# The message stage of a two-layer graph network: GpSimd issues its scatters and gathers by pairs of blocks

## What is computed

```python
h = jnp.maximum(_layernorm(x, axis=-1), 0.0)
src_full = jnp.concatenate([src, dst])
dst_full = jnp.concatenate([dst, src])
ef_full = jnp.concatenate([ef, ef], axis=0)
edge_in = jnp.concatenate([nf[src_full], nf[dst_full], ef_full], axis=-1)
msg = leaky_relu(edge_in @ We1) @ We2
red = jax.ops.segment_sum(msg, dst_full, num_segments=nf.shape[0])
node_in = jnp.concatenate([nf, red], axis=-1)
out_nf = leaky_relu(node_in @ Wn1) @ Wn2
```

## Time and profile before

| | |
|---|---|
| median of 3 runs | 5537.8 us |
| lowest and highest | 5531.38 and 5540.8 us |
| the profiled execution: its time | 5538.13 us |
| its span, first to last instruction | 5536.3 us |
| GpSimd (POOL) busy in the span | 3890.5 us (70%) |
| VectorE (DVE) busy | 3895.1 us (70%) |
| TensorE (PE) busy | 3325.0 us (60%) |
| ScalarE (ACT) busy | 1426.1 us (26%) |
| TensorE's granted clock, mean | 0.795 of full speed |
| scatters of the message stage, L1529 | 831, 1323.0 us, mean 1592 ns |
| gathers of the message stage, L1543 | 832, 828.4 us, mean 996 ns |
| the queue of GpSimd's transfers (q0) | 396.10 MB, 35.3% of the 16 DMA engines' span |

### The profile page before, as it was taken

How to read it: one execution, slowest core, us unless ns; L and a number is a source line. 1 busy time by engine, 2 the same in 40 slices (tenths; PEclk the granted TensorE clock), 3 DMA queues, 4 the chain that set the end, 5 groups by cost and what they waited for, 6 DMA issues and landing times. The chain is left out here.

```text
span 5536.3 us, 106419 instructions
## 1 busy us (share of the span) xinstructions
PE 3325.0 (60%) x16923; PEld 2273.1 (41%) x16924; DVE 3895.1 (70%) x11905; ACT 1426.1 (26%) x2966; POOL 3890.5 (70%) x3803
## 2 busy tenths in 40 slices
PE   0062222222156676244687877877887878778868
PEld 0031111111046665233354554545555545455537
DVE  4635555555578888887587777777777777777765
ACT  0130000000056666433322222222222222222222
POOL 3127777777679999721378888888878787888870
PEclk9685555555567778577899999999999999999989
DMA  2266666666256666412688888888888888888874
GB/s 57 60 182 194 193 196 192 194 194 193 81 126 153 154 155 154 150 42 76 183 183 182 179 180 179 180 179 179 178 177 182 177 180 177 180 179 182 177 144 141
DMA packets 725012, 891.72 MB, mean 161 GB/s; under 512 B 123241, under 2 KB 555465, under 8 KB 724710
## 3 DMA queue, kind: packets, MB, share of 16 engines
q0 software_dynamic: 217200, 396.10, 35.3%
q1 hardware_dynamic: 450742, 392.89, 24.9%
q10 hardware_dynamic: 56976, 101.87, 6.0%
HBM read 652.36 MB, written 238.06 MB: 161 GB/s over the span
## 5 line engine op out<-in xcount | busy, mean ns | idle before, releaser
L1529 POOL DMA_INDIRECT sums<-msg_bsum,k_sidx x831 | 1323.0, 1592 | 285.5 <-issue 241.7
L731 POOL DMA_INDIRECT max_xe<-rows,l_index x832 | 800.6, 962 | 426.6 <-issue 253.3
L1543 POOL DMA_INDIRECT msg_ga<-ab,k_bsrc x832 | 828.4, 996 | 368.7 <-issue 200.1
L1631 ACT ACTIVATE msg_low_ps<-msg_xs 128x512 f32<-128x512 f32 x928 | 558.0, 601 | 1986.8 <-DVE msg_xs L1600 1971.6
L1666 PEld LDWEIGHTS msg_both_ps<-msg_onehot,msg_hid 128*128 128x128 f32 x3712 | 552.0, 206 | 1216.7 <-DVE msg_bsum L1573 688.0
L1679 PE MATMUL msg_pre_ps<-msg_rw,msg_lt 128*128 128x512 f32 x1856 | 1030.0, 638 | 8.9 <-DMA msg_rw<-ab 8.9
L1666 PE MATMUL msg_both_ps<-msg_onehot,msg_hid 128*128 128x64 f32 x3712 | 616.4, 292 | 511.6 <-DVE msg_bsum L1573 500.4
L942 POOL TENSOR_SCALAR att_keyhot<-k_ramp,att_keys 128x128 f32<-128x128 f32 x1028 | 702.0, 703 | 56.1 <-ACT att_keys L1014 54.5
L1610 DVE TENSOR_TENSOR msg_hid<-msg_xs,msg_low_ps 128x512 f32<-128x512 f32 x928 | 634.5, 684 | 88.4 <-ACT msg_low_ps L1631 69.9
L1668 PE MATMUL msg_both_ps<-msg_hid,msg_same 128*128 128x256 f32 x1856 | 654.3, 437 | 0.0
L1599 DVE TENSOR_TENSOR msg_xs<-msg_pre_ps,msg_ga 128x256 f32<-128x256 f32 x928 | 388.9, 419 | 362.4 <-issue 157.4
(11 more groups left out here) (292 smaller groups left out, 5351.3 us busy)
## 6 DMA issues: line engine op xcount, KB each, us to landing
msg_rw<-ab SPq DMA_DIRECT2D x928, 128.0 KB
l_outside<-xe SPq DMA_DIRECT2D x1028, 72.0 KB, 2.7
xe<-max_xe SPq DMA_DIRECT2D x104, 576.0 KB, 3.0
max_src<-srcs ACTq DMA_DIRECT2D x104, 512.0 KB, 3.8
att_keyrow<-key ACTq DMA_DIRECT2D x257, 128.0 KB, 3.5
msg_lt<-in_efT SPq DMA_DIRECT2D x928, 32.0 KB
rows<-node_rows SPq DMA_DIRECT2D x50, 288.0 KB, 2.4
max_begin<-begin ACTq DMA_DIRECT2D x104, 128.0 KB, 2.5
```

Source lines behind the costliest of these rows:

```text
L731: pool.indirect_dma_start(xe[:, b, u, :], None, T.rows, bass.IndirectOffsetOnAxis(ap=K.index[:, k:k + 1], axis=0)).then_inc(s_xe[b], 16)
L1529: pool.indirect_dma_start(T.sums[k % 2], bass.IndirectOffsetOnAxis(ap=K.sidx[:, k:k + 1], axis=0), bsum[:, (k + 1) % SB, :], None, compute ...
L1543: pool.indirect_dma_start(ga[:, (k + 1) % RB, :], None, T.ab, bass.IndirectOffsetOnAxis(ap=K.bsrc[:, k:k + 1], axis=0)).then_inc(s_ga[k % ...
L1631: act.activation(low_ps[u % 2][:, :], xs[:, u % 2, :], ACT.Copy, scale=SLOPE1).then_inc(s_low, 1)
```

## The change

In the message stage GpSimd's loop goes over pairs of blocks. For k and k + 1 it issues both scatters, then passes both landings, then issues both gathers. What each of the three does, and all its counts, stay as they are. The three statements for one k become three loops over the pair:

```diff
             pool.sem_inc(s_sent, SB)
-            for k in range(NB + RB):
-                if RB <= k < BLOCKS + RB:
-                    scatter(k - RB)
-                if LEAD <= k < NB + LEAD:
-                    landed(k - LEAD)
-                if k < NB:
-                    pool.indirect_dma_start(ga[:, (k + 1) % RB, :], None, T.ab,
-                                            bass.IndirectOffsetOnAxis(ap=K.bsrc[:, k:k + 1], axis=0)).then_inc(s_ga[k % 4], 16)
+            def gather(k):
+                pool.indirect_dma_start(ga[:, (k + 1) % RB, :], None, T.ab,
+                                        bass.IndirectOffsetOnAxis(ap=K.bsrc[:, k:k + 1], axis=0)).then_inc(s_ga[k % 4], 16)
+
+            for first in range(0, NB + RB, 2):
+                pair = (first, first + 1)
+                for k in pair:
+                    if RB <= k < BLOCKS + RB:
+                        scatter(k - RB)
+                for k in pair:
+                    if LEAD <= k < NB + LEAD:
+                        landed(k - LEAD)
+                for k in pair:
+                    if k < NB:
+                        gather(k)
```

## The result

The change makes the kernel slower: 5554.1 us in the median of 7 runs (5551.0 to 5556.6) against 5537.8 for the kernel before, also 7 runs (5531.4 to 5542.4), a ratio of 1.0028 with a 95% interval of 1.0016 to 1.0039. That is 16 us more, where 15 us less was forecast.

A forecast was written before the change was run, and what follows sets the result against it. The prediction took GpSimd, never resting, to bound the message stage. Its terms, -30.6 + 9 + 4 + 3 = -14.6 us from the profiled 5538.1, less 0.3 to the median, gave 5523 us, range 5503 to 5546.

The forecast's parts named there:

- What bounds the kernel: Message stage: GpSimd never rests, 2597 of 2620 us with issue; VectorE is the next bound at about 2458 us.
- Durations, -30.6 us: Steady message stage: second gather 47 ns and second scatter 28 ns shorter, 75 ns a pair over 408 pairs, -30.6 us.
- The low end: Lower bound of the saving from shorter second instructions in the message stage: 0, if something else made those rows shorter.
- Issue, 0: GpSimd in the message stage: 0.30 us before each instruction, whether kinds repeat or alternate; change 0.
- The scatters' wait, +9: Scatter waiting for the scatter two before: distance falls from 6.38 to 6.30 us, a seventh of 815 late, +9 us.
- The first gather's wait, +4: First gather of a pair waits for the first of the pair before, 6.30 us instead of 9.6: +4 us.
- The head, +3: Start of the message stage: first eight pairs each wait for the pair before, first scatter starts later, +3 us.
- Other waits, 0: Message stage and tail: waits for block sums, s_sent and s_got, SyncE's loads and the tail cost nothing more, 0.
- the queue's case: Shared DMA queue backs up when gathers come two by two, landings late: 5576 us; slower by over 11 us, chance 0.13.
- The first rival: Message stage: order carries no price, nothing saved, 5545 us; chance 0.27, shared with the forecast with larger waits.

The follow-up runs named there:

- quads: The change with runs of four, four scatters then four gathers, and a landing lead of four instead of three: 5907.3 us, one run.
- before_memset: The kernel before with a 128x1 memset on GpSimd ahead of each gather: 5543.0 us, one run.
- before_plain: The kernel before with scatters that overwrite instead of adding, so the backward sums are left out: 5372.7 us, one run.
- extra_gather: The kernel before with a second, small gather (128 rows of 128 bytes from another table) behind each gather: 6647.4 us, one run.

## Why the prediction was wrong

The durations that the order sets, as medians of the trace over its steady part (some 180 to 810 instructions each; in ns):

| order | scatter: 1st, 2nd, 3rd, 4th of a run | gather: 1st, 2nd, 3rd, 4th | two blocks |
|---|---|---|---|
| one and one (before) | 1589 | 994 | 5166 |
| two and two (the change) | 1625, 1577 | 1019, 984 | 5205 |
| four and four | 1625, 1580, 1556, 1554 | 1017, 982, 947, 947 | 5104 |
| forecast for two and two | 1589, 1561 | 994, 947 | 5091 |

- **What bounds the kernel**: right. GpSimd bounds the message stage before and after; in the change it is idle for little more than 0.30 us an instruction, and with it freed VectorE takes over near the forecast place (5372.7 us). VectorE's wait for s_sent didn't shrink (167.4 us after 162.4), because GpSimd did not get faster.
- **Durations, -30.6 us**: the step that failed, and with its sign; it measured +17. The prediction took "47 ns for the second gather of a pair and 20 to 37 ns, taken as 28, for the second scatter", with "firsts unchanged". Two errors lie in it. The short gathers came from long runs, sixteen at the head and the 832 of the maxima with nothing between them. The tail gave 1.57 us for a second scatter and 1.55 for a third, and the 28 ns lie between the two. In the change a second one is only part of the way down: 984, not 947; 1577, not 1561. And the first of a run was not 1589 and 994 but 1625 and 1019, since two of the other kind had run before it. In the rows of before no scatter or gather of the steady part has two of the other kind ahead of it. Only the very first scatter has, 1.63 us after sixteen gathers; it stood in the earlier trace rows, and the prediction takes nothing from it. From -30.6 to +17 is 48 us, and the whole miss, from -15 to +15, is only 30: the scatters' wait and the head were wrong as well, by 14 and 4 us the other way.
- **The low end**, "0, if something else made those rows shorter", was no low end. The term needed a bound on the other side of zero too: fewer switches between the kinds, each one dearer.
- **Issue, 0**: right, 0.30 us between all.
- **The scatters' wait, +9**: -5. The distance grew from 6.38 to 6.41 us instead of shrinking. That a seventh of the scatters would be late rested on one row of seven. Between 2740 and 5350 us of before's trace, 54 of 811 start over 0.05 us late, one in fifteen; in the change 32 of 806. With the same distance and the looser lead it is 49 of 807, so the -5 may be no more than what one trace differs from another.
- **The first gather's wait, +4**: the size came out, +4, and the looser lead took it away. It lies in 11 late gathers, not in a little of each. That such a wait is not free is shown twice: by this idle time, and by the 250 us lost at a distance of 4.5. In before's trace a gather's last semaphore update comes 3.25 to 6.61 us after its start, 3.91 in the median, over the 672 of the steady part whose updates are all recorded.
- **The head, +3**: -1; the pairs were permitted 4.1 to 5.1 us apart, where the rows had 5.03 to 5.89. **Other waits, 0**: right.
- **The rivals**: the queue's case had the right side by the wrong mechanism; late landings cost no more than was forecast. The first rival would have left 5545 us and the durations alike; they are not. A price that every instruction pays alike, as the 0.30 us before each in both orders, is not what differs here. A rival with a real price for two in a row was missing, and 5554 lay 8 us outside the range.

That the order of kinds has a price was shown: with the waits of pairs and a lead of four, one and one stands at 0.9999 of before and two and two at 1.0020. That the price falls with fewer switches was an extrapolation from long runs to runs of two. The measured price of two blocks goes up first, from 5166 to 5205 ns at runs of two, and is down to 5104 at runs of four. Runs of three were not run; by the rows for four they would be at 5138 (an estimate: 1625 + 1580 + 1556 + 1017 + 982 + 947 = 7707, by 3, times 2).

Why the first of a run is dearer stays open. It is not time (a 3 us wait in a run changes nothing), not the table or row size of what ran before, not the sequencer's batches, and a memset does not bring it about. No run here shows what inside GpSimd sets it.

## What to carry to other kernels

An instruction's price read at the end of a long run of its own kind is not the price of the second in a row (here 947 against 984 ns for a gather); look for rows with exactly the history that the new order will give it, and where there is none, bound the term on both sides of zero. Where GpSimd's indirect DMAs are the bound (80% busy here, and 0.30 us before each), an order of kinds was worth its tens of nanoseconds here only in runs of four (runs of three by an estimate), and then the landings that the order brings together (same table, same buffer) have to be moved apart first. The distance from issue to the wait for the landing is the other half of such an order: at 6.4 us it cost 4 us in all here, at 4.5 us 250.

## What the runs showed of the hardware

- An indirect DMA on GpSimd took 36 (scatter with add) and 47 ns (gather) over its shortest median, 1553 and 947 ns, after one of the other kind (before); 72 and 72 after two, and then 24 and 37 for the second (after); 72 and 70 after four, and then 27 and 35 (quads). A memset of 128x1 between them cost neither anything (1588 and 991 ns, before_memset).
- Adding made up 600 of a scatter's 1593 ns on GpSimd, for 128 rows of 1 KB (993 without it, before_plain). 128 rows of 128 bytes cost a gather 951 ns as second after one scatter (extra_gather), 128 rows of 2 KB 947 as third and fourth of a run (quads), so row size counted for little.
- A memset of 0.68 us on GpSimd ran beside the end of an indirect DMA, not after it, as the trace of before_memset has it (4002.39 to 4003.07, with the scatter until 4002.95).
- At the head of the stage (before) the first gather was busy on GpSimd until 2691.05 us; the first packet of its queue q0 started at 2691.77, 0.72 us later.
- From its start to its last semaphore update a gather of 256 KB took 3.25 to 6.61 us, 3.91 in the median, with the DMA engines 83% busy; a scatter with add of 128 KB 3.68 to 6.06, 4.18 in the median (672 and 704 of before's).
- After a late landing GpSimd's next instruction started 0.97 us (scatter; 0.968 to 0.982 in 41 late ones of before) or 0.83 us (first gathers of the change, 0.829 to 0.840 in ten late ones) after its sequencer had passed the wait. So of a distance of 4.5 us some 3.5 us are left for the landing (an estimate, 4.5 - 0.97), less than the median gather takes.
